# The triangular inverse in 64 by 64 cells, a new order of steps, and table loads issued later

## What is computed

```
q, k, v = silu(causal_conv4(x @ W*))          # q, k normalised per head
A = (k*beta) @ k.T                             # 64 x 64 per chunk, all heads summed
T = (I + tril(A, -1)) ^ -1                     # written in the reference as a loop over 64 rows
W, U = T @ (k*beta), T @ (v*beta)
```

## Time and profile before

| what | value |
|---|---|
| median of 3 executions | 835.7 us |
| span of the profiled execution | 835.2 us |
| TensorE busy | 690.9 us (83%) |
| VectorE busy | 451.4 us (54%) |
| ScalarE busy | 365.3 us (44%) |
| GpSimd busy | 530.1 us (63%) |
| first scatter of rows starts | 98.75 us |
| last scatter of results starts | 774.76 us |

### The profile page before, as it was taken

The page is one execution under the profiler, slowest core; times in us unless marked ns, Lnnn a source line. Parts: engine busy times, 40 slices in busy tenths (PEclk is TensorE's granted clock), DMA queues, the critical chain, the costliest instruction groups (busy, mean ns, idle before and its releaser), DMA issues.

```text
span 835.2 us, 16706 instructions
## 1 busy us (share of the span) xinstructions
PE 690.9 (83%) x5000; PEld 600.3 (72%) x5000; DVE 451.4 (54%) x1487; ACT 365.3 (44%) x917; POOL 530.1 (63%) x552
## 2 busy tenths in 40 slices
PE   5689898989898987766899989979988987970495
PEld 3567676777677766543778989979988987970485
DVE  2246868676867676646665644534443433430384
ACT  1445454636454544241234664654644554430032
POOL 0000277777777777777777777777777777777231
PEclk9899999989998989967599999999997999895598
DMA  8202041414141413112544444444443444311795
GB/s 208 80 1 93 12 153 61 153 60 153 61 153 60 141 61 114 61 60 77 149 123 124 112 121 124 127 122 122 126 119 110 124 110 127 92 53 53 299 407 211
DMA packets 89946, 98.49 MB, mean 118 GB/s; under 512 B 21675, under 2 KB 73603, under 8 KB 89859
## 3 DMA queue, kind: packets, MB, share of 16 engines
q1 hardware_dynamic: 67043, 58.45, 24.5%
q0 software_dynamic: 20992, 37.78, 13.2%
q10 hardware_dynamic: 1824, 1.20, 0.5%
HBM read 55.03 MB, written 42.34 MB: 117 GB/s over the span
## 4 chain that ended last, share of the span: by engine, by line
PE 52%; DVE 11%; issue 8%; POOL 8%; DMA 8%; ACT 6%; SPq 5%; ACTq 0%; POOLq 0%; DVEq 0%
POOL y_dram L482 8%; PE pb L1179 5%; PE pa L1179 5%; PE fc L1154 4%; PE ba L1378 4%; DMA arena<-y_dram 4%; PE fc L1399 3%; PE fb L1399 3%; PE fb L1154 3%; DMA y_dram<-arena 3%; PE fa L1159 3%; PE bb L1378 3%; SPq L411 3%; PE ba L1159 2%; PE pa L1399 2%
## 5 line engine op out<-in xcount | busy, mean ns | idle before, releaser
L458 POOL DMA_INDIRECT rows_dram<-rows x256 | 253.6, 990 | 176.4 <-issue 173.8
L482 POOL DMA_INDIRECT y_dram<-arena x272 | 261.3, 961 | 83.5 <-issue 73.1
L651 ACT ACTIVATE arena<-weights 128x176 f32 x384 | 99.1, 337 | 11.0 <-DVE arena L1035 10.3
L640 ACT ACTIVATE arena<-fb 88x512 f32<-88x512 f32 x39 | 23.1, 593 | 100.9 <-PE fc L1399 90.8
L1179 PE MATMUL pa<-tap,xc 128*128 128x384 f32 (+1 forms) x128 | 54.6, 557 | 9.3 <-DVE tap L948 9.3
L1154 PEld LDWEIGHTS fc<-arena 128*128 128x128 f32 x384 | 48.6, 193 | 16.0 <-ACT arena L547 10.5
L1089 DVE TENSOR_TENSOR arena<-ba,arena 128x512 f32<-128x512 f32 x34 | 23.5, 691 | 67.0 <-DMA y_dram<-arena 52.6
L1154 PE MATMUL fc<-arena 128*128 128x128 f32 x384 | 52.1, 279 | 8.1 <-ACT arena L547 7.3
L1159 PE MATMUL fa<-const,arena 128*128 128x128 f32 x296 | 47.3, 284 | 9.5 <-DMA arena<-rows_dram 4.2
L1378 PE MATMUL bb<-weights,arena 88*128 x336 | 47.8, 293 | 7.3 <-DVE arena L1124 6.0
L1378 PE MATMUL ba<-weights,arena 88*128 x304 | 41.6, 286 | 14.7 <-DVE arena L1124 13.4
(11 more groups left out here) (293 smaller groups left out, 1469.7 us busy)
## 6 DMA issues: line engine op xcount, KB each, us to landing
arena<-y_dram SPq DMA_DIRECT2D x16, 1024.0 KB, 11.9
arena<-rows_dram SPq DMA_DIRECT2D x192, 76.0 KB
weights<-experts SPq DMA_DIRECT2D x16, 608.0 KB, 6.5
arena<-rows_dram SPq DMA_DIRECT2D x128, 38.0 KB
y_dram<-arena POOLq DMA_INDIRECT x272
rows_dram<-rows POOLq DMA_INDIRECT x256, 2.3
xc<-x_chan SPq DMA_DIRECT2D x8, 256.0 KB, 3.8
x_res<-x_tok SPq DMA_DIRECT2D x8, 256.0 KB, 2.8
```

The costliest lines, as they stand in the source:

```text
L458: pool.indirect_dma_start(rows_dram, bass.IndirectOffsetOnAxis(ap=slot_of(a)[:, i, k:k + 1], axis=0), rows[:, NT * a + i, :], None).then_i ...
L482: pool.indirect_dma_start(y_dram, bass.IndirectOffsetOnAxis(ap=go_to[:, t:t + 1], axis=0), y_sb[q % YRING][:, i, :], None).then_inc(ys[q % ...
L640: act.activation(sil_t[m % 2][0:I, :], gate_of(m)[0:I, :], ACT.Silu).then_inc(S.sil_done, 1)
L651: ins = act.activation(w_here[n % 2][:, (parts(q) * i + h) * 2 * I:(parts(q) * i + h + 1) * 2 * I], weights[:, bass.ds(at[i], 2 * I)], ACT ...
```

## The change

**Cells.** T, its transpose and the level products are kept as 64 x 64 cells: partitions 0 to 63 hold the first chunk of each tile and 64 to 127 the second, with 64 columns per tile (256 per batch instead of 512). `at` and `aa` become one step `at` of 16 products of 128 rows by 64 columns, `z{k}` 8 cell products, `inv{k}` 16 (T and its transpose both, so `invt{k}` with its turns is gone), `xk` and `tr` 8 each. Halves alternate: a cell product on rows and columns 0 to 63 of the array is followed by one on 64 to 127, and both write the same PSUM bank.

**Mask on a factor.** The mask moves from the result (`cp{k}`) to the factor: VectorE's `zc{k}` copies z under the mask into a buffer `z_eye[k]` that already holds an identity (256 columns); ScalarE's `ic{k}` and `itc{k}` copy T and its transpose (256 columns). `eye` is gone; GpSimd writes all identities once, at the start. `cp0` is two masked copies, the second of which also waits for `nat`.

```diff
-                    tiles(fa, lambda i: blk(k_chan, i), lambda i: blk(kb_chan, i)).then_inc(S.at_mm, 1)
+                    for ps, lhs, rhs in ((fa, k_chan, kb_chan), (fc, kb_chan, k_chan)):
+                        for i in range(NT):
+                            for half in range(2):
+                                at = (2 * i + half) * C
+                                mm = pe.matmul(cell(ps, i, half), lhs[:, at:at + C], rhs[:, at:at + C], start=True, stop=True)
...
-                        tiles(fc, lambda i: blk(inv_t[n], i), lambda i: blk(z_sb, i)).then_inc(S.inv_mm, 1)
+                        older = inv_t0 if k == 1 else inv_t[n]
+                        cells(fc, older, z_eye[k]).then_inc(S.inv_mm, 1)
+                        cells(fa, z_eye[k], older).then_inc(S.invt_mm, 1)
...
+            def cells(ps, lhs, rhs):
+
+                for i in range(NT):
+                    for half in range(2):
+                        mm = pe.matmul(cell(ps, i, half), cell(lhs, i, half), cell(rhs, i, half), start=True, stop=True)
...
-                        dve.copy_predicated(by_tile(inv), mask_of(k, 0), by_tile(fc[:, :])).then_inc(S.inv_done, 1)
+                        dve.copy_predicated(by_chunk(z_eye[k]), mask_of(k), by_chunk(fb[:, 0:NT * C])).then_inc(S.z_done, 1)
...
+            pool.wait_ge(S.consts_in, 16)
+            for ap in (lev0, z_first, z_later):
...
+                ins = pool.tensor_copy(by_chunk(ap), const[:, K_EYE:K_EYE + C].unsqueeze(1).broadcast_to([P, n, C]))
```

```diff
-            sp.dma_start(mask[:, :, :], masks).then_inc(S.masks_in, 16)
+            sp.wait_ge(S.conv_in, 16 * 7)
+            sp.dma_start(masks_flat[:, 0:(LEVELS + 1) * C], masks).then_inc(S.masks_in, 16)
...
+            act.wait_ge(S.conv_in, 16 * 7)
             act.dma_start(const[:, :], consts).then_inc(S.consts_in, 16)
```

More of the change, by code:

```diff
@@ L83 @@
 K_SINK = K_CHUNK + 4
[L84 to L101, removed]
@@ L167, in block_program @@
         squares, p1, p2 = part(1024), by_tile(part(512)), by_tile(part(512))
-        neg_a_t, z_sb, inv, k_chan, kb_chan, dot_out, z2 = (part(512) for _ in range(7))
+        k_chan, kb_chan, dot_out, z2 = (part(512) for _ in range(4))
+        neg_a_t, inv = part(NT * C), part(NT * C)
+        lev0 = part(2 * NT * C)
+        inv_t0, inv0 = lev0[:, 0:NT * C], lev0[:, NT * C:2 * NT * C]
+        masks_flat = mask[:, :, :].rearrange("p n c -> p (n c)")
+        z_first, z_later = part(NT * C), masks_flat[:, (LEVELS + 1) * C:(LEVELS + 1) * C + (LEVELS - 2) * NT * C]
+        z_eye = [None, z_first] + [z_later[:, k * NT * C:(k + 1) * NT * C] for k in range(LEVELS - 2)]
         g_sb = by_tile(part(512))
@@ L171, in block_program @@
         kb, vb = ([by_tile(part(512)) for _ in range(2)] for _ in range(2))
-        inv_t = [part(512) for _ in range(2)]
+        inv_t = [part(NT * C) for _ in range(2)]
         t1, t2, o_sb = (by_tile(part(512)) for _ in range(3))
@@ L1155, in tiles, with spread_by @@
                 return mm
+            def cells(ps, lhs, rhs):
+                for i in range(NT):
+                    for half in range(2):
+                        mm = pe.matmul(cell(ps, i, half), cell(lhs, i, half), cell(rhs, i, half), start=True, stop=True)
+                return mm
+            def spread_by(ps, lhs, rhs):
+                for i in range(NT):
+                    for half in range(2):
+                        mm = pe.matmul(half_of(ps, i, half), cell(lhs, i, half), rhs(i, half), start=True, stop=True)
+                return mm
             def turned(ps, src):
@@ L1196, in steps @@
                         pe.wait_ge(S.decay_done, a)
[L1197 to L1207 removed]
+                        pe.wait_ge(S.inv_done, (LEVELS - 1) * a)
@@ L1208, in steps @@
+                    for ps, lhs, rhs in ((fa, k_chan, kb_chan), (fc, kb_chan, k_chan)):
+                        for i in range(NT):
+                            for half in range(2):
+                                at = (2 * i + half) * C
+                                mm = pe.matmul(cell(ps, i, half), lhs[:, at:at + C], rhs[:, at:at + C], start=True, stop=True)
+                    mm.then_inc(S.at_mm, 1)
                 for k in range(1, LEVELS):
                     if op == f"z{k}":
-                        if a >= 1 and k == 1:
-                            pe.wait_ge(S.g_done, a)
@@ L1243, in steps @@
                         pe.wait_ge(S.x1_done, a)
-                    tiles(bb, lambda i: blk(inv_t[n], i), lambda i: t1[:, i, :]).then_inc(S.tr_mm, 1)
+                    spread_by(bb, inv_t[n], lambda i, half: t1[half * C:(half + 1) * C, i, :]).then_inc(S.tr_mm, 1)
                 if op == "to":
```

174 lines of the change are left out of this document (112 added, 62 removed).

## The result

The changed kernel is slower: 850.9 us median (849.6 to 851.8) against 835.9 for the kernel before on the same chip, a ratio of 1.017 with a 95% interval of 1.0155 to 1.0183. Forecast were 832 and "faster". The profiled execution has a span of 850.0 us, 14.8 longer than before.

What follows compares the result with a forecast made beforehand. GpSimd's scatter stream was taken as the bound: first scatter 98.75 + stream 677 + tail 59.5 = 835.2 us. An earlier start (-5.4) and a new stall (+1.7) gave -3.7: span 831.5, median 832, range 822 to 862.

Steps and rivals of the forecast that it cites:

- first scatter + stream + tail: Whole span of the kernel before: GpSimd's first scatter at 98.75, its stream 677, the tail 59.5, together 835.2 us.
- side by side cells: TensorE's cell products: the two halves of the array overlap, 0.056 us per cell; 0.112 if in turn.
- rival 1: TensorE's halves run in turn at 0.112 us per cell: 878 us, or 845 to 895 by price; chance 0.20.
- The place of the first new wait: GpSimd's scatter 4 waits for `kt` of batch 2: a new stall of 1.7 us, bounds 0 and 4.
- the walk of a batch: One later batch stepped from `xk` to `xk`: 38.4 us, 41.0 with half clock, against GpSimd's 41.6, so no stall.
- The margin to 41.6: Later batches: TensorE's round of 41.0 us stays just below GpSimd's 41.6, so GpSimd does not stall.
- Rival 2: Cells side by side, but low clock lasts longer: batches of 42 to 43.5 us, 835 to 846 in all; chance 0.14.
- The start: Batch 0 up to GpSimd's first scatter: at 93.3 us, 5.4 earlier than before.
- plus 0.4 of half-speed clock: Batch 0 from `xk.0` to `tanh.0`: sparser TensorE work at lower clock adds 0.4 us, within a stretch of 25.7.
- g, p1, p2 and sum1 of batch 1 (2.3) ... go in between: Batch 0 from `tanh.0` to `key2.0`: these batch 1 steps add 2.3 us, within a stretch of 15.9.
- The loads: Kernel start: later tables give 1.2 us, ScalarE's wait for constants takes back 0.7; net -0.5, bounds -1.5 and +2.
- quad 8: Expert stage: no GpSimd gap beyond 0.3 us expected near it, as TensorE's path there moves earlier too.

Runs made afterwards that it cites:

- run 5: Changed kernel plus nine products per batch that nothing reads, for batches 1 to 6, placed where TensorE stood idle: 840.2 us.
- Run 13: Changed kernel with two of the four projection taps left out in batches 2 to 7, every wait and the order kept: 833.1 us.
- run 11: Changed kernel with `x1t`, `logits` and `tanh` of batch 0 moved ahead of pieces they stood behind: 850.6 us.
- Run 6: Changed kernel's cells and late loads in the old order, with projection pieces, silu steps and some inverse copies moved into the freed room: 833.9 us.
- run 12: Run 6 with GpSimd's waits for TensorE between the row scatters off, the waits for the rows' own data kept: 828.4 us.
- run 3: Kernel before with only the loads changed: masks, tables and constants issued after the seven projection weights: 835.2 us.
- run 10: Changed kernel with, for batches 2 to 6, the next batch's head and a later projection piece put between `cs` and `res`: 856.1 us.

## Why the prediction was wrong

**Right.** The method: first scatter + stream + tail, GpSimd's stream as the frame, nothing moving in the expert stage's 343 us or the tail. The side by side cells (0.065 against 0.056 forecast, and about 0.10 when the order of issue prevents it, where 0.112 was forecast). The Trainium skill (TensorEngine Tiling, Restrictions and Gotchas) says that different row tiles cannot access one PSUM bank at once; by that rule rival 1 should have come. Here both halves write one bank and 8 cells take 0.52 us, so this trace does not show that limit. The place of the first new wait: scatter 4, released by a turn into `pa`, 2.6 us over the usual gap where 1.7 was forecast, within its bounds of 0 and 4.

**The step that failed** is the walk of a batch and what hangs on it: "VectorE's router sets it, not TensorE's sum. With the clock at half during the sparse part (some 2.6 us) it is 41.0, just below GpSimd's 41.6: no stall". The round is 44.3. Three columns, counted in us from the end of `xk.1` (136.3 in the changed kernel, 131.3 in run 5):

| step | walked, full clock | changed kernel | run 5, clock 1.00 |
|---|---|---|---|
| `tr` | 8.2 | 7.9 | 7.3 |
| `kt` | about 12 | 13.4 | 11.9 |
| `z1` | 17.0 | 20.0 | 17.0 |
| `logits` | 24.1 | 27.4 | 24.4 |
| `rank` | 36.1 | 41.1 | 38.0 |
| end of the next `xk` | 38.4 | 44.3 | 41.2 |

Up to `z1` run 5 is as walked, and the changed kernel 3.0 late: that is the clock, for which 2.6 was booked. From `z1` on both need 24.3 us, and 21.4 was walked: 2.9 that the sum had at nothing. Most of it, 2.6, comes behind `logits`, where TensorE is never idle up to the end of `xk` (16.9 us in both, 14.3 walked). So there TensorE's sum sets the round and not VectorE's router, and the prediction shows no such sum. Of the 2.6 three projection pieces at 1.49 and three at 1.39 in place of 1.3 make 0.8, 72 cells at 0.065 in place of 0.056 make 0.6, and the remaining 1.2 is not parted by any run. Run 13 bears it out: with less projection work the round falls by 3.1. The margin to 41.6 was 0.6 us; the clock alone would have used up 0.4 of it, the rest put the round over it, and the error comes back in each batch. GpSimd's rounds 0 to 5 take 44.3 us (99.05 to 364.94), 2.75 more than the 41.56 of before, and the last two 40.9, 0.6 less each: 6 x 2.75 - 1.2 = 15.3.

Rival 2 ("side by side, but the order is too thin") named half of the mechanism and its place, with a chance of 0.14, and priced it at 42 to 43.5 per batch and 835 to 846. The measured 44.3 and 850.9 lie beyond both ends, for the dearer work of TensorE behind `logits` wasn't in it.

**The start** was forecast 5.4 us earlier and came 0.3 later, 5.7 off. Its terms: `xk.0` ends at 52.85 (51.3 forecast, 58.4 before), 1.5 late, though a gain of 5.6 was there. From there to `tanh.0` 28.8 (25.7), then 16.4 to the end of `key2.0` (15.9), then 1.0 to the scatter (0.4). The largest error is in the second, and its failed term is "plus 0.4 of half-speed clock": in run 5, with the clock up there, the same stretch takes 26.1 (51.05 to 77.20), so the low clock costs 2.7. "g, p1, p2 and sum1 of batch 1 (2.3) ... go in between" was nearly right, 0.5 short with the rest of its term. Shortening the router's chain on TensorE alone gave nothing (run 11), since `zc4.1` stands in VectorE's queue and waits for TensorE's full one. Run 6, whose order has `g.1` and what follows it behind the keys, has its first scatter at 90.88.

**Would the start have mattered?** Little. In run 6 the first scatter is 7.9 us earlier than before, and at batch 1 2.6 are left (138.40 against 140.97): what GpSimd gains over TensorE's rounds it gives back at the next wait. It keeps it only where TensorE's rounds are no longer than its own and those waits are off (run 12).

**The loads** were booked at -0.5, after taking 0.7 off 1.2 for ScalarE; run 3 shows the whole 1.2. The expert stage stayed as forecast, without a gap at quad 8 in the changed kernel, where GpSimd comes 15 us later.

**Open.** How the 2.9 us behind `z1` divide between row changes, cells and the rest; whether a better order of the new kind exists (run 10 was one try); why GpSimd's scatters take 1.4 us more per batch in run 5 than in the changed kernel.

## What to carry to other kernels

When two engines run in rounds of almost the same length, the difference of the rounds is the result, and each error in it counts once per round: walk the round at the clock that the trace shows for sparse stretches, add up the whole queue of an engine that works in order beside the chain that seems to lead, and price each change of shape. Faster products give time only if the order that a planner or a hand wrote for the slow ones is retimed around them (843.5 against 833.9), and if nothing that the bound engine waits for stands behind a wait for another batch. Where an engine is paced by waits for another, try the kernel without them once the other's rounds are no longer than its own.
